# Masked attention: the query tiles in mixed order, the values' products in one stretch per two units

## The chip, the core and the metric

The kernel runs on one core of a Trainium2 chip. Its time is the device time of one execution in microseconds (us). Three runs took 3441.07, 3441.09 and 3444.06 us, median 3441.09.

Engines in this text: PE is the matrix engine, DVE the vector engine, ACT the engine for activations, POOL the general one, SP the one that issues DMAs. Each works through its own list of instructions in program order, and waits at semaphores that the others raise.

## The reference

The program is two layers over 1250 rows (nodes, later tokens) of 512 numbers: a graph sum, attention with a mixture of experts, a second graph sum, and a block with a temporal attention, a spatial attention, a cross attention and an MLP. Four attentions in all; the temporal one alone is masked:

```python
def _temporal_experts(xt, idx, qw, qb, kw, kb, vw, vb, pw, pb):
    B, T, _ = xt.shape                      # 1, 1250; H = 8 heads of HD = 64
    q = (jnp.einsum('btd,bod->bto', xt, qw[idx]) + qb[idx][:, None, :]).reshape(B, T, H, HD)
    ...
    logits = jnp.einsum('bthd,bshd->bhts', q, k) * HD ** (-0.5)
    causal = jnp.tril(jnp.ones((T, T), dtype=bool))
    logits = jnp.where(causal, logits, -jnp.inf)
    att = jax.nn.softmax(logits, axis=-1)
    o = jnp.einsum('bhts,bshd->bthd', att, v).reshape(B, T, D)
    o = jnp.einsum('btd,bod->bto', o, pw[idx]) + pb[idx][:, None, :]
    return xt + o
```

## The kernel before

`attention` is called four times, once with `causal=True`. After the projections it works through 80 units. A unit is one head and one tile of 125 queries; the heads go in 4 pairs, and a pair has 20 units. The order is in `units` (L593): for each pair, tiles two by two (0 and 1, then 2 and 3, ...), and for each two tiles both heads. So four units in a row see the same number of keys. Under the mask that number, `keys` (L594), is 2, 4, 6, 8 or 10 tiles of 125 keys, growing through the pair. Without the mask it is always 10.

Steps of a unit, and who takes them:
- PE multiplies queries and keys (`score_part`, L771 and L773, two products per piece). A unit has up to three pieces, in the order of `pieces` (L590). The scores of an even and of an odd unit lie in five banks, and share the middle one: an odd unit's last piece, and the last of an even unit with 10 tiles, wait for the exponential of the unit before (L770, `exp_done`).
- DVE adds the mask to the last one or two tiles (L960; 250 wide for an even unit, 125 for an odd one) and takes the maximum of the row (L962). Both are in `whole_max`. The stages without mask take most of the maximum ahead of time (`wide_max`, L968) and the last 226 columns later (`tail_max`, L975).
- ACT exponentiates with that maximum and sums up (L904).
- PE turns the result tile by tile (`turn_part`, L790), at most four tiles to a bank, which gives one, two or three turns per unit. ACT (L890) or DVE (L986) copies each turn to `p_t`; `by_act` says who.
- Two units next to each other (same head, two tiles) share one sum with the values: `duo_sum` (L807), for which one product of 250 columns per key tile is issued (the trace has two records for each). Even and odd key tiles go to the two halves of a bank. ACT copies the lower half (L914), DVE adds it to the upper and writes the output (L1008).

All engines step together through s = 0, 1, 2, ...: in step s PE makes the scores of unit s and turns units s-2 (or s-1), DVE takes the maximum of s-1 and its copies of s-2, ACT exponentiates s-1. When masked, each step holds two quarters of a sum between score pieces, and the half copy and the add come in odd steps (`sum_at`, L600). When not masked, PE works in two kinds of steps: an even one with turns and scores, and an odd one with scores, turns and then one whole sum ahead of the last score piece.

After a few units the sums of the exponentials are inverted (`norms`, L610: three times per pair), sent through DRAM to be spread over partitions (SP, L676 and L682), and POOL multiplies the output with them (`scale`, L712), the last time DVE.

Of the kernel before, what the change touches and what calls it, by code (L numbers as in the profile page):

```python
# [27 lines left out]
D = 512  # L28
TN = 125
NT = N // TN  # L30
DC = D // 128
# [11 lines left out]
HEADS = 8  # L43
# [458 lines left out]
def attention(nc, c, q_src, kv_src, out_t, wq_d, wk_d, wv_d, bq_d, bk_d, scratch, causal=False, pick=None, send=None,  # L502
# [10 lines left out]
    with ExitStack() as ctx:  # L513
# [76 lines left out]
        pieces = [[(0, 512), (512, 1024), (1024, N)], [(TAIL, TAIL + 512), (TAIL + 512, N), (0, TAIL)]]  # L590

        w_out = k_hi_both[:, :, :].rearrange("p h n -> p (h n)")[:, 0:DC * D].rearrange("p (k d) -> p k d", k=DC)
        units = [(j, h, i) for j in range(PAIRS_) for m in range(0, NT, 2) for h in range(2) for i in (m, m + 1)]  # L593
        keys = [(i // 2 * 2 + 2 if causal else NT) for _, _, i in units]  # L594
        turns = [-(-n // 4) for n in keys]
        upto = lambda u: sum(turns[:u])

        taken = [(u, n) for u in range(NU) for n in range(turns[u])]
        by_act = lambda u, n: (n == 0 or (n == 2 and u % 2 == 0)) if causal else (n == 2) == (u % 2 == 0)
        sum_at = lambda s: (s - 5) // 2 if causal and s % 2 == 1 else (s - 6) // 2 if not causal and s % 2 == 0 else -1  # L600
        act_by = lambda g: sum(1 for u, n in taken[:g] if by_act(u, n))
        dve_by = lambda g: g - act_by(g)

# [3 lines left out]
            if dve_by(g):  # L607
                eng.wait_ge(dve_took, dve_by(g))

        norms = [(j, k) for j in range(PAIRS_) for k in range(3)]  # L610
        n_units = lambda j, k: (UNITS * j + 8 * k, UNITS * j + min(8 * k + 8, UNITS))
        with stage(nc, "bias_in", "bias_set", "s_high", "s_low", "w_in0", "w_in1", "w_high", "w_low", "summed", "high",
                   "low", "saved", "first_in", "kq_in0", "kq_in1", "scored", "wide_scored", "wide_ready", "masked", "max_ready", "exp_done",
                   "turned", "act_took", "dve_took", "pv_done", "half_out", "added", "inv_made", "inv_out", "inv_in",
# [73 lines left out]
            @block.gpsimd  # L688
            def _(pool):
                if send is not None:  # L690
                    table_d, rows, slots = send

                def send_rows(a, b):
                    for t in range(a, b):
                        pool.indirect_dma_start(table_d, bass.IndirectOffsetOnAxis(ap=slots[:, t:t + 1], axis=0),  # L695
                                                rows[:, t, :], None).then_inc(sent, 16)

                first = 20 if send is not None else 0
                for n, (kind, last) in enumerate((("k", begin[1]), ("q", begin[5]))):
                    send_rows(first * n, first * (n + 1))  # L700
                    for r in range(RINGS):
                        pool.wait_ge(stored[r], stores_by(last, r))
                    load_pair(pool, 0, kind, first_in)

                def scale(x):
                    j, k = norms[x]
                    lo, hi = CHUNKS[k]
                    pool.wait_ge(inv_in, 32 * (x + 1))
                    pool.wait_ge(added, NT * j + min(4 * k + 4, NT))
                    dst = out_t[:, j, lo:hi].rearrange("q (i p) -> q i p", p=TN)  # L710
                    by = inverse_all[:, 0:hi - lo].rearrange("q (p i) -> q i p", p=TN)
                    pool.tensor_tensor(dst, dst, by, ALU.mult).then_inc(scaled, 1)  # L712

                early_norms = len(norms) - 3
                for x in range(len(norms) - 1):
                    if send is not None:
                        end = lambda n: 2 * first + (EC - 2 * first) * min(n, early_norms) // early_norms
                        send_rows(end(x), end(x + 1))
                    scale(x)
                pool.wait_ge(scaled, len(norms) - 1)  # L720
                if send is not None:
                    pool.wait_ge(sent, 16 * EC)

            @block.tensor
            def _(pe):
# [88 lines left out]
                for s in range(NU + 4):  # L814
                    if s == 2:

                        pe.wait_ge(low, len(items))
                    if causal:
                        quarter = 2 * (s % 2)
                        turn_part(s - 2, 0)  # L820
                        score_part(s, 0)
                        turn_part(s - 2, 1)
                        duo_sum((s - 4) // 2, quarter, quarter + 1)
                        score_part(s, 1)
                        turn_part(s - 2, 2)
                        duo_sum((s - 4) // 2, quarter + 1, quarter + 2)
                        score_part(s, 2)
                    elif s % 2 == 0:
                        turn_part(s - 2, 0)
                        turn_part(s - 2, 1)  # L830
                        score_part(s, 0)
                        score_part(s, 1)
                        turn_part(s - 2, 2)
                        turn_part(s - 1, 0)
                        score_part(s, 2)
                    else:
                        score_part(s, 0)
                        score_part(s, 1)
                        turn_part(s - 2, 1)
                        turn_part(s - 2, 2)  # L840
                        duo_sum((s - 5) // 2, 0, 4)
                        score_part(s, 2)

            @block.scalar
            def _(act):
# [46 lines left out]
                                   ACT.Copy).then_inc(act_took, 1)  # L892

                act.wait_ge(w_low, len(parts))
                for s in range(NU + 4 if causal else NU + 5):
                    take_part(s - 2, 0)
                    if 1 <= s <= NU:
                        t = s - 1
                        act.wait_ge(max_ready, t + 1)
                        if t >= 2:  # L900

                            act.wait_ge(turned, upto(t - 1))
                        w = TN * keys[t]
                        act.activation(p[:, t % 2, 0:w], score[t % 2][0:TN, 0:w], ACT.Exp,  # L904
                                       bias=neg_max[:, t:t + 1], accum_out=total[:, t:t + 1]).then_inc(exp_done, 1)
                    take_part(s - 2, 1)
                    take_part(s - 2, 2)
                    if sum_at(s) >= 0:
                        q = sum_at(s)
                        act.wait_ge(pv_done, q + 1)  # L910
                        if q >= 2:

                            act.wait_ge(added, q - 1)
                        act.activation(lower[:, q % 2, :], pout[64:128, 0:2 * TN], ACT.Copy).then_inc(half_out, 1)  # L914

            @block.vector
            def _(dve):
# [68 lines left out]
                    dve.tensor_copy(p_t[:, u // 2 % 2, 4 * n:4 * n + m, TN * (u % 2):TN * (u % 2) + TN],  # L986
                                    pturn[0:TN, g % 2, 0:TN * m].rearrange("p (a b) -> p a b", b=TN)).then_inc(dve_took, 1)

                for s in range(NU + 4 if causal else NU + 5):
                    if 1 <= s <= NU:  # L990
                        (whole_max if causal else tail_max)(s - 1)
                    u = s - 2
# [16 lines left out]
                                          lower[:, q % 2, :], ALU.add).then_inc(added, 1)  # L1009
                dve.wait_ge(added, NU // 2)  # L1010
                j, k = norms[-1]
                lo, hi = CHUNKS[k]
                dve.wait_ge(inv_in, 32 * len(norms))
                dst = out_t[:, j, lo:hi].rearrange("q (i p) -> q i p", p=TN)
                by = inverse_all[:, 0:hi - lo].rearrange("q (p i) -> q i p", p=TN)
# [1312 lines left out]
def program(nc, a, out):  # L2328
# [5 lines left out]
    with ExitStack() as ctx:  # L2334
# [26 lines left out]
        support, x1, z2 = (rows(n) for n in ("support", "x1", "z2"))  # L2361
        y_moe = dram("y_moe", [EXPERTS, CAP, D])
        scratch = (dram("q_parts", [2, HEADS // 2, 128, N]), dram("k_parts", [2, HEADS // 2, 128, N]),
                   dram("inverse", [3 * HEADS // 2, 2, 4 * TN]), dram("w_out", [128, DC, D]))
        hold = lambda: nc.sbuf_tensor(f"x_sb_{nc.next_id()}", [TN, NT, D], F32, side="right")
        with ExitStack() as layer0:
            s0 = lambda name, shape, dt=F32: layer0.enter_context(nc.sbuf_tensor(name, shape, dt))
# [132 lines left out]
```

## Time and profile before

| | |
|---|---|
| median of three runs | 3441.09 us |
| profiled execution, its span | 3439.76 us, 3437.5 us |
| busy share of the span: PE, DVE, ACT, POOL | 83%, 56%, 42%, 32% |
| mean granted PE clock | 0.928 of 2.4 GHz |
| HBM | 119 GB/s |
| exponentials, all attentions (L904) | 320, busy 383.8 us |
| turns by PE (L790), records | 2880, busy 433.6 us |
| products with the values (L807), records | 2880, busy 355.3 us |
| maxima of the masked stage (L962) | 80, 417 to 1460 ns |

The busy time of PE is modelled at its end, so that a PE that is marked busy need not be at its peak. A window's clock column is the mean of what was granted. In the timeline a row may stand for several instructions of one kind (x8); the number after the start is then the time from the first's start to the last's end.

### The profile page before, as it was taken

Reading aid. Unit: us, or ns where it says so; the run is one execution under the profiler, and the core shown is the slowest. Engines: PE = TensorE matmul, PEld = TensorE weight load, DVE = VectorE, ACT = ScalarE, POOL = GpSimd, SP = SyncE. Lnnn points to the kernel's source line nnn. Section 1 sums busy time; section 2 is a strip of 40 time slices with the busy share of each in tenths; the row PEclk is TensorE's granted clock in tenths of the full one; section 3 lists DMA queues with packets and bytes.
Section 4 is the critical chain, followed back from the end, with each engine's and each line's share of the span. In section 5 each row is a group of like instructions: output and inputs, shape, how many; then the busy total and the mean of one; then the engine's idle time right before and its main releaser. Section 6 shows DMA issues by size and latency. Waiting matters only on the chain. (4 is left out here: it accounts for less than half of the span.)

```text
span 3437.5 us, 46642 instructions
## 1 busy us (share of the span) xinstructions
PE 2854.2 (83%) x15398; PEld 1999.1 (58%) x15398; DVE 1925.7 (56%) x3890; ACT 1457.2 (42%) x3150; POOL 1115.2 (32%) x1138
## 2 busy tenths in 40 slices
PE   0403887999958995779999798989999999998899
PEld 0201227777756763434444585558777687776687
DVE  7203774577642114579999526653677636776544
ACT  0100003466604542556666435542566435665322
POOL 4777775467113433076665000000000000001220
PEclk9856998999968997989999899999999999999999
DMA  4104775533156994454443264214423044321322
GB/s 109 36 6 114 210 202 160 138 61 72 40 161 212 339 341 125 162 172 150 138 136 92 79 191 107 56 58 129 129 54 67 15 146 113 73 48 41 98 75 87
DMA packets 228769, 407.93 MB, mean 119 GB/s; under 512 B 48706, under 2 KB 146288, under 8 KB 224438
## 3 DMA queue, kind: packets, MB, share of 16 engines
q1 hardware_dynamic: 173222, 268.49, 27.3%
q0 software_dynamic: 54864, 136.39, 14.8%
q8 instruction: 127, 2.08, 0.3%
q14 instruction: 108, 0.88, 0.1%
q10 hardware_dynamic: 448, 0.08, 0.0%
HBM read 318.32 MB, written 90.35 MB: 119 GB/s over the span
## 5 line engine op out<-in xcount | busy, mean ns | idle before, releaser
L904 ACT ACTIVATE at_p<-at_pb,at_max 125x1250 f32<-125x1250 f32 (+4 forms) x320 | 383.8, 1199 | 302.0 <-DVE at_unused L975 273.3
L790 PE MATMUL at_pb<-ident,at_p 125*125 125x125 f32 x2880 | 433.6, 281 | 20.8 <-ACT at_p L904 17.6
L790 PEld LDWEIGHTS at_pb<-ident,at_p 125*125 125x125 f32 x2880 | 391.2, 191 | 83.7 <-ACT at_p L904 22.0
L807 PE MATMUL at_pb<-at_pt,at_v 125*64 125x250 f32 x2880 | 355.3, 383 | 5.2 <-DVE s_t L1008 3.0
L1457 PE MATMUL so_ps<-g_got,g_hot 128*125 128x512 f32 x332 | 177.5, 630 | 204.8 <-DMA g_got<-support,g_edges 172.0
L968 DVE TENSOR_REDUCE at_wide<-at_pb 125x1 f32<-125x1024 f32 x240 | 293.6, 1223 | 22.1 <-PE at_pb L773 3.8
L890 ACT ACTIVATE at_pt<-at_pb 125x500 f32<-125x500 f32 (+1 forms) x448 | 232.8, 520 | 97.4 <-PE at_pb L790 93.5
L712 POOL TENSOR_TENSOR s_t<-s_t,at_all 128x500 f32<-128x500 f32 (+1 forms) x33 | 42.7, 1293 | 656.2 <-DVE s_t L1008 656.0
L807 PEld LDWEIGHTS at_pb<-at_pt,at_v 125*64 125x64 f32 x2880 | 188.2, 137 | 104.1 <-issue 14.4
L750 PE MATMUL at_pb<-at_s,at_shared 128*128 128x500 f32 (+1 forms) x1152 | 229.2, 361 | 23.2 <-ACT at_shared L852 23.2
L986 DVE COPY at_pt<-at_pb 125x500 f32<-125x500 f32 (+1 forms) x416 | 232.4, 582 | 22.6 <-PE at_pb L790 22.6
L1457 PEld LDWEIGHTS so_ps<-g_got,g_hot 128*125 128x125 f32 x332 | 50.6, 187 | 331.7 <-issue 197.9
L695 POOL DMA_INDIRECT table<-rows,slots x160 | 197.9, 1237 | 95.7 <-issue 57.5
L750 PEld LDWEIGHTS at_pb<-at_s,at_shared 128*128 128x128 f32 x1152 | 196.0, 194 | 55.9 <-ACT at_shared L852 23.9
L1414 POOL DMA_INDIRECT table<-rows,slots x160 | 195.4, 1221 | 99.1 <-issue 99.1
L975 DVE TENSOR_SCALAR_CACHE_REDUCE at_unused<-at_pb,at_wide 125x226 bf16<-125x226 f32 x240 | 107.7, 449 | 205.3 <-PE at_pb L773 202.5
L2147 POOL DMA_INDIRECT g_got<-nodes,g_edges x176 | 176.9, 1005 | 133.7 <-DMA g_edges<-table 103.5
L2173 PE MATMUL g_pw<-g_w4two,g_h 128*128 128x512 f32 x352 | 181.4, 599 | 22.1 <-DMA g_h<-h_edges 17.7
L2184 PE MATMUL g_pm<-g_msg,g_hot 128*125 128x512 f32 x352 | 187.8, 615 | 14.3 <-DVE g_acc L2269 7.1
L771 PE MATMUL at_pb<-at_kh,at_q 128*125 128x512 f32 (+5 forms) x448 | 179.3, 407 | 20.0 <-ACT at_p L904 18.4
L2187 PE MATMUL g_pm<-g_msg,g_plain 128*125 128x512 f32 x352 | 181.4, 597 | 0.0
L771 PE MATMUL at_pb<-at_shared 128*125 128x512 f32 (+5 forms) x448 | 177.0, 402 | 3.9 <-ACT at_p L904 3.2
(320 smaller groups left out, 5505.7 us busy)
## 6 DMA issues: line engine op xcount, KB each, us to landing
w_ring<-in_L_ffn_w SPq DMA_DIRECT2D x128, 512.0 KB, 11.7
at_shared<-k_parts SPq DMA_DIRECT2D x64, 312.5 KB
ml_w<-in_mlp_w SPq DMA_DIRECT2D x64, 256.0 KB
k_parts<-at_shared SPq DMA_DIRECT2D x64, 250.0 KB, 2.9
q_parts<-at_shared SPq DMA_DIRECT2D x64, 250.0 KB, 3.4
h_edges<-em_both SPq DMA_DIRECT2D x11, 1024.0 KB, 3.9
g_h<-h_edges SPq DMA_DIRECT2D x11, 1024.0 KB, 5.6
at_shared<-q_parts SPq DMA_DIRECT2D x32, 312.5 KB
```

Source lines behind the costliest of these rows:

```text
L695: pool.indirect_dma_start(table_d, bass.IndirectOffsetOnAxis(ap=slots[:, t:t + 1], axis=0), rows[:, t, :], None).then_inc(sent, 16)
L750: ins = pe.matmul(bank[:, (x + 6) % 8, 0:s.stop - s.start], a[:, ci % 2, k, 128 * (j % 2):128 * (j % 2) + 128], b[:, k, s], start=(t == 0) ...
L771: pe.matmul(score[u % 2][0:TN, a:b], q_two[j % 2][h][:, TN * i:TN * i + TN], k_hi[j % 2][h][:, a:b], start=True, stop=False)
L790: ins = pe.transpose(pturn[0:TN, g % 2, TN * (t % 4):TN * (t % 4) + TN], p[:, u % 2, TN * t:TN * t + TN], c.ident[0:TN, 0:TN])
L807: ins = pe.matmul(pout[side:side + 64, 0:2 * TN], v[:, t, 2 * j + h, :], p_t[:, q % 2, t, :], start=(t < 2), stop=(t >= keys[u] - 2))
L890: act.activation(p_t[:, u // 2 % 2, 4 * n:4 * n + m, TN * (u % 2):TN * (u % 2) + TN], pturn[0:TN, g % 2, 0:TN * m].rearrange("p (a b) -> p ...
L904: act.activation(p[:, t % 2, 0:w], score[t % 2][0:TN, 0:w], ACT.Exp, bias=neg_max[:, t:t + 1], accum_out=total[:, t:t + 1]).then_inc(exp_d ...
L968: dve.tensor_reduce(neg_wide[:, u:u + 1], score[u % 2][0:TN, a:a + 1024], AX, ALU.max, negate=True)\
L986: dve.tensor_copy(p_t[:, u // 2 % 2, 4 * n:4 * n + m, TN * (u % 2):TN * (u % 2) + TN], pturn[0:TN, g % 2, 0:TN * m].rearrange("p (a b) -> ...
L1414: pool.indirect_dma_start(self.table_d, bass.IndirectOffsetOnAxis(ap=self.slots[:, t:t + 1], axis=0), self.rows[:, t, :], None).then_inc(s ...
L1457: pe.matmul(ps[0:TN, 4 + i % 4, :], self.hot[:, i % HOT, :], self.got[:, i % RING, :], start=True, stop=True)\
L2184: pe.matmul(pm[0:TN, 2 * (q % 2), :], hot[:, t % MR, :], msg[:, t % MR, 0:4, :].rearrange("p a b -> p (a b)"), start=not second, stop=bool ...
```

## The change

Only for the masked attention the order of the query tiles becomes 8, 0, 6, 2, 4, so that the key tiles per unit go 10, 2, 8, 4, 6 in groups of four units. The masked stage drops its own order of steps and takes that of the others: whole sums in odd steps, the half copy and the add in even steps, and copies dealt by `(n == 2) == (u % 2 == 0)`: of an even unit DVE copies the turns 0 and 1 and ACT turn 2, of an odd unit the reverse. Each group has an inversion of its own, five per pair, and the number of steps is one more on ACT and DVE. For the other three attentions the lists come out as they were.

```diff
-        units = [(j, h, i) for j in range(PAIRS_) for m in range(0, NT, 2) for h in range(2) for i in (m, m + 1)]
+        groups = [(8,), (0,), (6,), (2,), (4,)] if causal else [(0, 2), (4, 6), (8,)]
+        order = [m for g in groups for m in g]
+        units = [(j, h, i) for j in range(PAIRS_) for m in order for h in range(2) for i in (m, m + 1)]
...
-        by_act = lambda u, n: (n == 0 or (n == 2 and u % 2 == 0)) if causal else (n == 2) == (u % 2 == 0)
-        sum_at = lambda s: (s - 5) // 2 if causal and s % 2 == 1 else (s - 6) // 2 if not causal and s % 2 == 0 else -1
+        by_act = lambda u, n: (n == 2) == (u % 2 == 0)
+        sum_at = lambda s: (s - 6) // 2 if s % 2 == 0 else -1
...
-        norms = [(j, k) for j in range(PAIRS_) for k in range(3)]
-        n_units = lambda j, k: (UNITS * j + 8 * k, UNITS * j + min(8 * k + 8, UNITS))
+        norms = [(j, k) for j in range(PAIRS_) for k in range(len(groups))]
+        until = lambda k: sum(len(g) for g in groups[:k])
+        n_units = lambda j, k: (UNITS * j + 4 * until(k), UNITS * j + 4 * until(k + 1))
+        n_columns = lambda k: (TN * groups[k][0], TN * (groups[k][-1] + 2))
...
-                    lo, hi = CHUNKS[k]
+                    lo, hi = n_columns(k)
...
-                    pool.wait_ge(added, NT * j + min(4 * k + 4, NT))
+                    pool.wait_ge(added, NT * j + 2 * until(k + 1))
...
-                    if causal:
-                        quarter = 2 * (s % 2)
-                        turn_part(s - 2, 0)
-                        score_part(s, 0)
-                        turn_part(s - 2, 1)
-                        duo_sum((s - 4) // 2, quarter, quarter + 1)
-                        score_part(s, 1)
-                        turn_part(s - 2, 2)
-                        duo_sum((s - 4) // 2, quarter + 1, quarter + 2)
-                        score_part(s, 2)
-                    elif s % 2 == 0:
+                    if s % 2 == 0:
...
-                for s in range(NU + 4 if causal else NU + 5):
+                for s in range(NU + 5):
```

The same names as above stand in the instruction lists; the lines of the changed kernel are 6 lower on DVE and 4 higher on PE. DVE before, in the 8-tile units: mask (250 wide is an even unit's), maximum, copy of a turn, add.

```order
L960 TENSOR_TENSOR at_pb<-at_pb,causal 125x125
L962 TENSOR_REDUCE at_max<-at_pb 125x1
L986 COPY at_pt<-at_pb 125x4x125
L960 TENSOR_TENSOR at_pb<-at_pb,causal 125x250
L962 TENSOR_REDUCE at_max<-at_pb 125x1
L986 COPY at_pt<-at_pb 125x4x125
L1008 TENSOR_TENSOR t_t<-at_pb,at_lower 64x250
L960 TENSOR_TENSOR at_pb<-at_pb,causal 125x125
L962 TENSOR_REDUCE at_max<-at_pb 125x1
```

DVE in the changed kernel, in the 8-tile units:

```order
L954 TENSOR_TENSOR at_pb<-at_pb,causal 125x250
L956 TENSOR_REDUCE at_max<-at_pb 125x1
L954 TENSOR_TENSOR at_pb<-at_pb,causal 125x125
L956 TENSOR_REDUCE at_max<-at_pb 125x1
L980 COPY at_pt<-at_pb 125x4x125 x2
L1002 TENSOR_TENSOR t_t<-at_pb,at_lower 64x250
L954 TENSOR_TENSOR at_pb<-at_pb,causal 125x250
L956 TENSOR_REDUCE at_max<-at_pb 125x1
```

The add (`t_t<-at_pb,at_lower`) stood ahead of the mask of an odd unit (125 wide) and stands ahead of that of an even one (250 wide), behind the even unit's two copies.

PE before, in the first 2-tile units of a pair, behind the 10-tile ones (`ident` rows are turns, `at_pt,at_v` products with the values, 24 and 226 wide rows the scores of an odd 2-tile unit):

```order
L790 MATMUL at_pb<-ident,at_p 125x125 x4
L771 MATMUL at_pb<-at_shared 125x24
L773 MATMUL at_pb<-at_shared 125x24
L790 MATMUL at_pb<-ident,at_p 125x125 x4
L807 MATMUL at_pb<-at_pt,at_v 64x250 x4
L771 MATMUL at_pb<-at_shared 125x226
L773 MATMUL at_pb<-at_shared 125x226
L790 MATMUL at_pb<-ident,at_p 125x125 x2
L807 MATMUL at_pb<-at_pt,at_v 64x250 x2
```

PE in the changed kernel at the same place:

```order
L775 MATMUL at_pb<-at_kh,at_q_24098 125x24
L777 MATMUL at_pb<-at_kl,at_q_24098 125x24
L775 MATMUL at_pb<-at_kh,at_q_24098 125x226
L777 MATMUL at_pb<-at_kl,at_q_24098 125x226
L794 MATMUL at_pb<-ident,at_p 125x125 x6
L811 MATMUL at_pb<-at_pt,at_v 64x250 x10
L794 MATMUL at_pb<-ident,at_p 125x125 x2
L775 MATMUL at_pb<-at_kh,at_q_24099 125x250
L777 MATMUL at_pb<-at_kl,at_q_24099 125x250
L794 MATMUL at_pb<-ident,at_p 125x125 x2
```

The ten products of a 10-tile sum stood in pieces of two and four between the scores; now they stand in one row, and the scores of the next unit behind them.

## Rows read from the trace of the kernel before

**Rows 1.** Timeline of ACT: exponentials; start us, us, line, operation, [idle before <-releaser]
```profile
2056.23 0.47 ACT L904 ACTIVATE at_p<-at_pb,at_max 125x250 f32<-125x250 f32 x1 [1.39 <-DVE at_max L962]
...
2112.25 0.47 ACT L904 ACTIVATE at_p<-at_pb,at_max 125x250 f32<-125x250 f32 x1
...
2122.57 0.67 ACT L904 ACTIVATE at_p<-at_pb,at_max 125x500 f32<-125x500 f32 x1
...
2133.74 0.88 ACT L904 ACTIVATE at_p<-at_pb,at_max 125x750 f32<-125x750 f32 x1
...
2144.68 1.09 ACT L904 ACTIVATE at_p<-at_pb,at_max 125x1000 f32<-125x1000 f32 x1
...
2150.72 1.09 ACT L904 ACTIVATE at_p<-at_pb,at_max 125x1000 f32<-125x1000 f32 x1
...
2157.99 1.30 ACT L904 ACTIVATE at_p<-at_pb,at_max 125x1250 f32<-125x1250 f32 x1 [0.87 <-DVE at_max L962]
...
2172.57 0.46 ACT L904 ACTIVATE at_p<-at_pb,at_max 125x250 f32<-125x250 f32 x1
...
2289.61 1.30 ACT L904 ACTIVATE at_p<-at_pb,at_max 125x1250 f32<-125x1250 f32 x1 [0.92 <-DVE at_max L962]
```

**Rows 2.** Windows: length, busy us of PE PEld DVE ACT POOL, PEclk, DMA, GB/s
```profile
2113.00:2173.00 60.00, 53.83 (x328) 35.08 (x326) 35.97 (x68) 33.58 (x72) 3.72 (x3) 0.94 0.37 76
2123.20:2133.20 10.00, 8.54 (x39) 5.91 (x38) 5.17 (x11) 4.62 (x13) 0.00 (x0) 0.70 1.03 219
2450.00:2700.00 250.00, 250.00 (x1820) 195.83 (x1819) 182.91 (x360) 161.26 (x280) 12.70 (x10) 1.00 0.22 48
```

**Rows 3.** Timeline between two exponentials, 8-tile unit, then a 10-tile one
```profile
2091.61 0.38 ACT L914 ACTIVATE at_lower<-at_pb 64x250 f32<-64x250 f32 x1
...
2092.02 0.41 DVE L1008 TENSOR_TENSOR t_t<-at_pb,at_lower 64x250 f32<-64x250 f32 x1 [0.57 <-ACT at_lower L914]
...
2092.36 0.28 DVE L960 TENSOR_TENSOR at_pb<-at_pb,causal 125x125 f32<-125x125 f32 x1
...
2092.67 1.20 DVE L962 TENSOR_REDUCE at_max<-at_pb 125x1 f32<-125x1000 f32 x1
...
2093.90 1.10 ACT L904 ACTIVATE at_p<-at_pb,at_max 125x1000 f32<-125x1000 f32 x1 [0.66 <-DVE at_max L962]
...
2095.20 0.37 PE L771 MATMUL at_pb<-at_kh,at_q 128*125 128x226 f32 x1
...
2095.71 0.43 DVE L960 TENSOR_TENSOR at_pb<-at_pb,causal 125x250 f32<-125x250 f32 x1 [1.26 <-PE at_pb L773]
...
2096.17 1.46 DVE L962 TENSOR_REDUCE at_max<-at_pb 125x1 f32<-125x1250 f32 x1
```

**Rows 4.** Groups by form, 2053 to 2302 us: busy, mean ns, idle before
```profile
L890 ACT ACTIVATE at_pt<-at_pb 125x500 f32<-125x500 f32 x64 | 37.8, 590 | 55.4 <-PE at_pb L790 55.4
...
L986 DVE COPY at_pt<-at_pb 125x500 f32<-125x500 f32 x32 | 21.5, 671 | 8.4 <-PE at_pb L790 8.4
```

**Rows 5.** Timeline of PE in the next, unmasked attention stage
```profile
2472.31 2.33 PE L807 MATMUL at_pb<-at_pt,at_v 125*64 125x250 f32 x20
...
2474.57 0.37 PE L771 MATMUL at_pb<-at_kh,at_q 128*125 128x226 f32 x1
...
2474.89 1.04 PE L790 MATMUL at_pb<-ident,at_p 125*125 125x125 f32 x8
...
2475.68 0.48 PE L771 MATMUL at_pb<-at_kh,at_q 128*125 128x512 f32 x1
...
2476.71 1.01 PE L790 MATMUL at_pb<-ident,at_p 125*125 125x125 f32 x6
```

**Rows 6.** Timeline of SP at the causal stage's end
```profile
2294.17 0.26 SPq L676 DMA_DIRECT2D inverse<-at_inv  x1
```

**Rows 7.** Timeline of ACT and DVE in the unmasked stage
```profile
2477.59 0.38 ACT L914 ACTIVATE at_lower<-at_pb 64x250 f32<-64x250 f32 x1
...
2478.05 0.40 DVE L1008 TENSOR_TENSOR s_t<-at_pb,at_lower 64x250 f32<-64x250 f32 x1
```

More of the change, by code:

```diff
@@ L987, in take_part @@
                                     pturn[0:TN, g % 2, 0:TN * m].rearrange("p (a b) -> p a b", b=TN)).then_inc(dve_took, 1)
-                for s in range(NU + 4 if causal else NU + 5):
+                for s in range(NU + 5):
                     if 1 <= s <= NU:
@@ L1011, in _ @@
                 j, k = norms[-1]
-                lo, hi = CHUNKS[k]
+                lo, hi = n_columns(k)
                 dve.wait_ge(inv_in, 32 * len(norms))
@@ L2363, in program @@
         scratch = (dram("q_parts", [2, HEADS // 2, 128, N]), dram("k_parts", [2, HEADS // 2, 128, N]),
-                   dram("inverse", [3 * HEADS // 2, 2, 4 * TN]), dram("w_out", [128, DC, D]))
+                   dram("inverse", [NT // 2 * HEADS // 2, 2, 4 * TN]), dram("w_out", [128, DC, D]))
         hold = lambda: nc.sbuf_tensor(f"x_sb_{nc.next_id()}", [TN, NT, D], F32, side="right")
```

## The prediction

> **What bounds the kernel now.** The order of reading was: the page's slices, to see that no engine is full over the whole span; then one stretch of the causal attention by windows; then its exponentials in the timeline; then the rows between two exponentials. The page's chain of waits ends in the MLP and says nothing here.
>
> Only one of the four attention stages changes: the causal one. For the others the new lists give the same order (0, 2, 4, 6, 8) in the same three groups. So the question is how long 80 units take. The first exponential starts at 2056.23 and the last at 2289.61: 233.38 us [rows 1]. A middle pair takes 60.32 us, from 2112.25 to 2172.57, split by the starts of its groups: the four 2-tile units 10.32 us, 4-tile 11.17, 6-tile 10.94, 8-tile 13.31, 10-tile 14.58. "n-tile" means n key tiles.
>
> In such a pair PE is marked busy for 53.8 of 60 us, DVE 36.0, ACT 33.6 [rows 2]. None is full: a serial loop sets the pace. [Rows 3] shows it for 8-tile units. ACT copies the lower half of a finished sum (2091.61), DVE adds it (2092.02), masks the next scores (2092.36), takes the maximum (2092.67, 1.20 us), ACT exponentiates (2093.90, 1.10 us). Then PE writes the last piece of the next unit's scores (2095.20), since that piece shares a bank with the unit just exponentiated; mask follows 0.51 us later. DVE and ACT work in program order, so whatever stands between two maxima on DVE is in the loop, if it is late.
>
> **Sizes used.** Exponential E = 0.47, 0.67, 0.88, 1.10, 1.30 us for 2, 4, 6, 8, 10 tiles [rows 1, 3]. Maximum M = 1.20 for 8, 1.46 for 10 tiles [rows 3], so 0.26 per two tiles: 0.94, 0.68, 0.42 for the smaller.
>
> **Part 1: copies by even and odd units, the add in even steps.** On each engine the new stream of steps is the one that the other three stages already have; they differ in the maximum. Before, the half copy and the add stand ahead of an odd unit's maximum, where DVE would wait for the last piece of scores anyway. Now they stand ahead of an even unit's maximum, behind the exponential of the odd unit (first order excerpt).
> - Odd unit now: exponential, 0.15 until the last piece (0.20 in [rows 3], where PE had other work until then), 0.51 to the mask, 0.31 to the maximum, M, 0.03. That is E + M + 1.00: 3.30 us for 8 tiles. Before it was 1.10, some 0.10 for reading out the sum, and 2.29 from the half copy to the next exponential: 3.49.
> - Even unit now: E + 0.10, half copy and add 0.75, mask 0.46 (0.15 more than the short one), M, 0.03, that is E + M + 1.34: 3.64 us for 8 tiles. Before, from start to start, 6.04 us per two (2144.68 to 2150.72), so 2.55 for it. Two units: 6.94 against 6.04.
> - For 10 tiles ACT also copies the even unit's third turn ahead of the half copy, 0.40: 1.30 + 1.46 + 1.34 + 0.40 = 4.50; odd 3.76. Without the add it would still be 4.40: the last piece now stands behind four transposes (0.49).
>
> DVE takes on 16 four-tile copies at 0.671 us (10.7 us) that cost ACT 0.590 (9.4) [rows 4]. For even 6- and 8-tile units both copies (0.67 + 0.41, or 1.34) lie beside the odd exponential and half copy (0.98 + 0.4, or 1.20 + 0.4), so I cost them at nothing there. In the 2- and 4-tile groups they are not covered; they are in part 2. Two more reciprocals a pair (0.17 us each) stand after an odd step's copies; hidden except once per pair. SP gets 8 more rounds of three inverse DMAs and POOL 20 products for 12: SP's wait for each round is shorter than the 12 us between two, the loads of a pair's keys and queries stand ahead of a pair's first round as before, and POOL is busy 3.7 of 60 us [rows 2]. Nothing.
>
> **Part 2: the values' products in one stretch, in mixed order.** A 10-tile sum in one stretch takes 2.26 us on PE (2472.31 to 2474.57, in a stage that has this order already) [rows 5]; scaled by the number of products, 8 tiles take 1.87 with a start of 0.1. Transposes: 0.125 each at 8 per 1.04; two 512-wide score pieces about 1.0 (2475.68 to 2476.71). In the new order the sums of the 10-tile units stand in the 2-tile group (second order excerpt), those of the 8-tile ones in the 4-tile group. Small units wait for them. From the start C of the first 2-tile exponential:
> - its end 0.62; last piece 0.55; six transposes 0.85; products 2.33: C + 4.35. Meanwhile the second unit, behind DVE's copy of the last turn (0.42), reciprocal, mask and maximum, starts at C + 3.4.
> - third unit: transposes and copy 0.72, add 0.38, mask 0.44, maximum and gap 0.45: C + 6.34. Its end and the last piece of the fourth begin at C + 6.96; products until C + 9.84.
> - first 8-tile unit: transposes 0.25, its scores 1.0, mask, maximum 1.20: C + 12.8.
>
> So this group takes 12.8 us against 10.32. The 4-tile group, by the same steps from K: last piece K + 0.82, 0.55, transposes 0.50, products until 3.74; transposes 0.5, copy 0.67, add 0.38, mask 0.44, maximum 0.68: third unit K + 6.5; fourth's last piece 7.3, products until 9.75, then 0.55 + 0.67 + 0.38 + 0.44 + 0.97: K + 12.75, against 11.17.
>
> The other groups, up to the first unit of the next: 10-tile 3.76 + 4.50 + 3.76 + 3.46 = 15.48 (14.58 before); 8-tile 3.30 + 3.64 + 3.30 + 3.12 = 13.36 (13.31); 6-tile 2.82 + 3.16 + 2.82 + 3.98 = 12.78 (10.94), the last being the step into a 10-tile unit behind four transposes.
>
> **The sum.** A pair: 12.8 + 13.36 + 12.75 + 12.78 + 15.48 = 67.2 us. First to last exponential: 4 x 67.17, less the 3.98 into the first unit and 0.1 for the third unit, which has no add before it: 264.6 us, 31.2 more. Start: the first maximum is over 10 tiles, 1.46 for 0.42: +1.0. End: before, the last inverse leaves at 2294.17, 4.56 us after the last exponential began, behind a 10-tile remainder; now 0.98 + 0.40 + 0.41 + 0.2 = 2.0, and the DMAs and the last product follow as before [rows 6]: -2.5. Together +29.7.
>
> **The clock.** I used full-clock durations. Before, a middle pair has a mean granted clock of 0.94, and the 4-tile group 0.70 [rows 2]: about 2 x 0.06 x 60 = 7.2 us at 1.2 GHz, in which PE does 3.6 us of work too slowly. If it falls as much now and all of it were in the loop, 4 x 3.6 = 14 us come on top; if none, 0. Before, it is in a group of small units that it fell; now the two small groups hold 8.4 us of dense products, so I take 3. The Trainium skill, "TensorE: Matmul & The Clock Gate", section "Loop structure matters more than you think", says that back-to-back matmuls keep the clock up, and it counts for this change: by it the 3 fall away and the kernel ends at 3471 us. The stage without gaps on PE, 250 of 250 us busy at 1.00 [rows 2], agrees; none of its rows shows what PE's gaps of some 2 us beside the small units will do.
>
> Profiled: 3439.76 + 32.7 = 3472.5. The median of the runs is 1.33 us above the profiled one: **3474 us**.
>
> **Rivals.**
> - *The mixing hides what it should.* Small units run in the shadow of the large ones' products, so that only the loops E + M + 1.00 and E + M + 1.34 are left: 10-tile 16.5, 8-tile 13.9, 6-tile 12.0, 4-tile 10.1, 2-tile 8.2, 60.7 a pair: 4 x 60.7 - 4.1 = 238.7, +5.3, with the ends +3.8, 3445. For it: PE's 53.8 busy us hold waits. Against: the products are ahead of the next unit's scores in PE's order, and 2.33 us is more than a small unit's whole loop.
> - *Faster, by the clock.* The same, and the clock stays at 1.00: 4 x 3.6 = 14 us back, 3431. It decides where PE is in the loop at low clock, which the 4-tile group's 11.17 us for 10.1 makes possible. Against: the even unit's add is late by the order alone.
> - *Slower still, by the clock.* PE idles some 2 us before each small unit's last piece. If the clock falls there, the products that follow double: 2 x 2.33 + 2 x 1.87 = 8.4 us a pair, +34, 3508.
> - *No change* could come if the add were not in the loop and the boundary waits were those of now; the stage with this order shows the add at 2478.05 after the half copy at 2477.59 [rows 7], late behind the odd exponential. I count it with the first rival.
>
> **How the numbers follow.** Forecast 0.82 (own range 3458 to 3490: 2 us a pair either way for the waits I could not see, and the clock's 0 to 14), first rival 0.05, faster rival 0.04, slower rival 0.09. Range 3452 to 3496: it leaves out most of the slower rival, the two rivals below, and the forecast's own tails, together about 0.2. What this measurement can tell from no change is about 0.2%, 7 us. Slower 0.91, same 0.05, faster 0.04.
>
> **What would show it.** In the changed profile: a middle pair of 67 us from exponential to exponential; 8-tile units alternating 3.3 and 3.6 us instead of 3.5 and 2.5; ahead of an even unit's mask DVE's add, and its idle time put down to the half copy of ACT; runs of 20 product records beside 2-tile units, with the next scores behind them; the first 8-tile exponential some 4.5 us after the last 2-tile one. It would be wrong if even units keep 2.5 us, if the 2-tile group takes 10 us or less, or if the clock column of the small groups leaves the range 0.7 to 1.0.

## The result, and the profile after

The changed kernel takes 3495.59 us (median of 4 runs, 3494.01 to 3499.01), the kernel before 3441.08 in the same comparison (3431.85 to 3444.06). By these medians it is slower by 54.5 us, a ratio of 1.0158; over the single runs of both the ratio is 1.0165, 95% interval 1.0153 to 1.0177. The profiled execution took 3496.39 us, 56.6 more than before. The forecast was 3474, the range ended at 3496. The direction was right, but the forecast had only 33 of the 55 us.

Profile after, timeline of ACT: the first and the last exponential of the masked stage, and the first of each group of four in the second pair. These answer to [rows 1].

```profile
2056.37 1.30 ACT L898 ACTIVATE at_p<-at_pb,at_max 125x1250 f32<-125x1250 f32 x1 [2.43 <-DVE at_max L956]
...
2126.51 1.30 ACT L898 ACTIVATE at_p<-at_pb,at_max 125x1250 f32<-125x1250 f32 x1 [1.52 <-DVE at_max L956]
...
2141.77 0.47 ACT L898 ACTIVATE at_p<-at_pb,at_max 125x250 f32<-125x250 f32 x1 [0.49 <-DVE at_max L956]
...
2158.80 1.09 ACT L898 ACTIVATE at_p<-at_pb,at_max 125x1000 f32<-125x1000 f32 x1 [1.04 <-DVE at_max L956]
...
2172.18 0.68 ACT L898 ACTIVATE at_p<-at_pb,at_max 125x500 f32<-125x500 f32 x1 [0.49 <-DVE at_max L956]
...
2189.33 0.89 ACT L898 ACTIVATE at_p<-at_pb,at_max 125x750 f32<-125x750 f32 x1 [0.68 <-DVE at_max L956]
...
2202.13 1.30 ACT L898 ACTIVATE at_p<-at_pb,at_max 125x1250 f32<-125x1250 f32 x1 [1.52 <-DVE at_max L956]
...
2348.51 0.89 ACT L898 ACTIVATE at_p<-at_pb,at_max 125x750 f32<-125x750 f32 x1 [1.60 <-DVE at_max L956]
```

From first to last it is 292.14 us, for 233.38 before; the sum had 264.6. A middle pair takes 75.62 us (2126.51 to 2202.13), where the prediction named 67 as a sign. The groups of the second pair take 15.26 (10-tile), 17.03 (2-tile), 13.38 (8-tile), 17.15 (4-tile) and 12.80 (6-tile). The forecast said 15.48, 12.8, 13.36, 12.75 and 12.78. Three of five are right within 0.25 us; both groups of small units are over 4 us too short in it.

Windows by those groups (length, busy us of PE, PEld, DVE, ACT, POOL, then the granted clock, DMA, GB/s), answering to [rows 2]:

```profile
2126.51:2141.77 15.26, 10.33 (x70) 7.55 (x66) 9.59 (x16) 8.80 (x16) 0.67 (x1) 1.00 0.71 145
2141.77:2158.80 17.03, 14.56 (x74) 9.41 (x74) 5.80 (x15) 4.35 (x13) 0.79 (x2) 0.70 0.58 112
2158.80:2172.18 13.38, 7.44 (x48) 5.64 (x48) 8.78 (x16) 7.16 (x14) 0.73 (x1) 1.00 0.11 10
2172.18:2189.33 17.15, 14.57 (x76) 9.76 (x76) 6.40 (x14) 5.49 (x14) 0.73 (x1) 0.70 0.09 9
2189.33:2202.13 12.80, 9.59 (x66) 7.21 (x66) 8.35 (x16) 6.11 (x13) 0.74 (x1) 1.00 0.08 11
```

The clock column tells the two kinds apart: 1.00 in the three groups that came out as worked out, 0.70 in the other two. The DMA column doesn't: the two slow groups have 0.58 and 0.09 in it. Nor does PE's share of busy time: the 8-tile group has 7.44 of 13.38 us at 1.00.

The steady loop, timeline of ACT and DVE for two 8-tile units, the odd one first; [rows 3] is the same place before:

```profile
2162.12 1.10 ACT L898 ACTIVATE at_p<-at_pb,at_max 125x1000 f32<-125x1000 f32 x1 [2.13 <-DVE at_max L956]
...
2163.33 0.38 ACT L908 ACTIVATE at_lower<-at_pb 64x250 f32<-64x250 f32 x1
...
2163.74 0.41 DVE L1002 TENSOR_TENSOR t_t<-at_pb,at_lower 64x250 f32<-64x250 f32 x1 [0.48 <-ACT at_lower L908]
...
2164.07 0.41 DVE L954 TENSOR_TENSOR at_pb<-at_pb,causal 125x250 f32<-125x250 f32 x1
...
2164.52 1.20 DVE L956 TENSOR_REDUCE at_max<-at_pb 125x1 f32<-125x1000 f32 x1
...
2165.75 1.09 ACT L898 ACTIVATE at_p<-at_pb,at_max 125x1000 f32<-125x1000 f32 x1 [1.00 <-DVE at_max L956]
```

Here the mechanism stands as forecast. The even unit's exponential begins 3.63 us after the odd one's (3.64 in the sum), and between them lie the half copy, the add, the mask and the maximum, one behind the other.

Timeline of PE at the second 2-tile unit, where the sum of 10-tile units stands; [rows 5] is such a sum at full clock:

```profile
2140.46 0.26 PE L777 MATMUL at_pb<-at_shared 128*125 128x24 f32 x1
...
2142.39 0.55 PE L775 MATMUL at_pb<-at_shared 128*125 128x226 f32 x1 [1.67 <-ACT at_p L898]
...
2142.94 1.49 PE L794 MATMUL at_pb<-ident,at_p 125*125 125x125 f32 x6
...
2144.36 4.35 PE L811 MATMUL at_pb<-at_pt,at_v 125*64 125x250 f32 x20
...
2148.64 0.48 PE L794 MATMUL at_pb<-ident,at_p 125*125 125x125 f32 x2
```

PE waits 1.67 us for the exponential, writes the last piece, makes six turns in 1.4 us, and then the 20 records of the sum take 4.35 us. At full clock they took 2.33. Windows of 2 us over the same place, with the columns of before:

```profile
2139.00:2141.00 2.00, 1.28 (x8) 1.02 (x8) 1.04 (x3) 1.80 (x5) 0.00 (x0) 1.00 1.02 210
2141.00:2143.00 2.00, 0.61 (x3) 0.62 (x4) 0.70 (x2) 0.84 (x3) 0.72 (x1) 0.67 1.05 225
2143.00:2145.00 2.00, 2.00 (x11) 1.61 (x12) 0.54 (x3) 0.59 (x1) 0.00 (x0) 0.50 0.98 210
2145.00:2147.00 2.00, 2.00 (x14) 1.10 (x12) 0.57 (x2) 0.56 (x2) 0.00 (x0) 0.50 1.09 238
2147.00:2149.00 2.00, 2.00 (x13) 0.99 (x10) 0.00 (x0) 0.24 (x1) 0.00 (x0) 0.63 1.00 206
```

The clock falls to 1.2 GHz (0.50) while PE waits and does not come back until the sum is nearly over. The next sum, at the fourth 2-tile unit, has a gap of 1.62 us ahead of it, takes 4.02 us and again runs mostly at 0.50. But not every such gap is followed by the low clock. At the same place of the first pair the gap is 1.63 us and the sum takes 2.33 us; the window 2078.71 to 2086.12 is at 1.00:

```profile
2080.34 0.37 PE L775 MATMUL at_pb<-at_kh,at_q 128*125 128x226 f32 x1 [1.63 <-ACT at_p L898]
...
2080.74 2.33 PE L811 MATMUL at_pb<-at_pt,at_v 125*64 125x250 f32 x20
```

So in this kernel too the same sum at the same place is fast when the clock is up.

The last inverse, timeline of SP, answering to [rows 6]:

```profile
2350.56 0.26 SPq L680 DMA_DIRECT2D inverse<-at_inv  x1
```

It leaves 2.05 us after the last exponential began, for 4.56 before; the sum had 2.0.

### The profile page after: what moved, and what is told of

It reads as the page before. It is cut to its first block and busy times, and to the rows that moved or that the text cites. A ratio compares the mean times of both kernels' runs of the same rounds, so it can differ in the third digit from the quotient of the medians.

```text
span 3494.3 us, 46685 instructions
## 1 busy us (share of the span) xinstructions
PE 2863.9 (82%) x15398; PEld 2017.0 (58%) x15398; DVE 1938.8 (55%) x3914; ACT 1449.6 (41%) x3134; POOL 1115.4 (32%) x1146
## 5 line engine op out<-in xcount | busy, mean ns | idle before, releaser
L811 PE MATMUL at_pb<-at_pt,at_v 125*64 125x250 f32 x2880 | 362.9, 400 | 4.1 <-DVE s_t L1002 3.0
L980 DVE COPY at_pt<-at_pb 125x500 f32<-125x500 f32 (+1 forms) x432 | 240.9, 585 | 70.2 <-PE at_pb L794 70.2
L811 PEld LDWEIGHTS at_pb<-at_pt,at_v 125*64 125x64 f32 x2880 | 203.7, 144 | 111.0 <-issue 25.9
L884 ACT ACTIVATE at_pt<-at_pb 125x500 f32<-125x500 f32 (+1 forms) x432 | 223.1, 517 | 74.7 <-PE at_pb L794 71.1
L775 PE MATMUL at_pb<-at_kh,at_q 128*125 128x512 f32 (+7 forms) x448 | 175.3, 399 | 40.5 <-ACT at_p L898 40.2
L775 PE MATMUL at_pb<-at_shared 128*125 128x512 f32 (+7 forms) x448 | 173.7, 395 | 24.5 <-ACT at_p L898 24.5
```

The source lines that it names most:

```text
L775: pe.matmul(score[u % 2][0:TN, a:b], q_two[j % 2][h][:, TN * i:TN * i + TN], k_hi[j % 2][h][:, a:b], start=True, stop=False)
L811: ins = pe.matmul(pout[side:side + 64, 0:2 * TN], v[:, t, 2 * j + h, :], p_t[:, q % 2, t, :], start=(t < 2), stop=(t >= keys[u] - 2))
L884: act.activation(p_t[:, u // 2 % 2, 4 * n:4 * n + m, TN * (u % 2):TN * (u % 2) + TN], pturn[0:TN, g % 2, 0:TN * m].rearrange("p (a b) -> p ...
```

## The experiments

All times but two, which are marked as one run, are medians beside the kernel before, which took 3439.5 to 3440.3 us in these comparisons. "A 2-tile group" is the time from the first exponential of four 2-tile units to the first of the next group.

**The mixed order alone.** The old steps of the masked stage are put back, the order stays:

```diff
-                    if s % 2 == 0:
+                    if causal:
+                        quarter = 2 * (s % 2)
...
+                        duo_sum((s - 4) // 2, quarter, quarter + 1)
...
+                    elif s % 2 == 0:
```

> The mixed order of query tiles alone: the masked stage keeps its old steps (quarters of a sum between score pieces, half copy and add in odd steps, old dealing of copies). Theory (the loss is the even units' late add, and the whole sums that run at half clock behind PE's gaps): neither is here, so most of the 56 us are not there: 3445 to 3455 us, a pair 60 to 62 us from exponential to exponential. Rival (the mixed order itself costs it, since small units stand behind large ones): 3475 us or more.

Measured: 3446.79 us, ratio 1.0024 (1.0014 to 1.0033). First to last exponential 238.9 us, a middle pair 60.8. The window of a 2-tile group (columns as above):

```profile
2127.49:2137.93 10.44, 9.36 (x61) 5.28 (x60) 5.65 (x14) 4.41 (x16) 0.00 (x0) 1.00 0.92 195
```

The order costs 7 us and no more. Of the 5.5 us from first to last exponential 4.4 are in the first pair (60.4 us for 56.0), where the old order began with 2-tile units that had no sum of larger units beside them (7.53 us for the group, 10.32 later); a middle pair takes 60.8 for 60.3. The clock is at 1.00 in every group: with quarters of a sum between score pieces and turns, PE's gaps in a middle pair are at most 1.27 us.

**The new steps alone.** Query tiles in the old order:

```diff
-        groups = [(8,), (0,), (6,), (2,), (4,)] if causal else [(0, 2), (4, 6), (8,)]
+        groups = [(0,), (2,), (4,), (6,), (8,)] if causal else [(0, 2), (4, 6), (8,)]
```

> The new steps alone: query tiles in the old order 0, 2, 4, 6, 8, five groups per pair. Theory: even units' loop E + M + 1.34 in all groups, and one slow group per pair (2-tile, with the sums of the 10-tile units at half clock, some 16.5 us where 12.3 were at full clock). First to last exponential 251 us at full clock, 264 with the half clock, for 233 before: 3470 us, 3457 if the clock stays. Rival (it is the mixed order): 3441 to 3448 us.

Measured: 3469.65 us, ratio 1.0089 (1.0073 to 1.0106). First to last exponential 262.3 us. The 2-tile group behind the 10-tile one:

```profile
2122.51:2138.32 15.81, 12.52 (x66) 8.33 (x66) 5.18 (x15) 4.35 (x13) 0.77 (x2) 0.71 0.49 99
```

Both parts of the loss are there with the steps alone: even units of 3.16 (6 tiles), 3.63 (8) and 4.37 us (10), and one slow group in each of the pairs 2 to 4 (15.1 to 15.9 us, 0.71 to 0.77). The 4-tile group has 0.84 there and takes 10.4 to 10.7 us. The two single effects, 30 and 7 us, do not make up the 55: together order and steps give a second slow group per pair, the 4-tile one with the 8-tile sums.

**The gap filled with products.** Ahead of the first score piece of an odd 2- or 4-tile unit, six products of 512 columns go into banks of the same unit:

```diff
+                    if causal and n == 0 and u % 2 and keys[u] <= 4:
+                        for _ in range(6):
+                            pe.matmul(score[1][0:TN, TAIL:TAIL + 512], q_two[j % 2][h][:, TN * i:TN * i + TN],
+                                      k_hi[j % 2][h][:, TAIL:TAIL + 512], start=True, stop=True)
```

> The changed kernel with PE's gap filled: ahead of the first score piece of each odd 2- and 4-tile unit six products of 512 columns are added, into a part of the same unit's score banks that is written again or not read. They need about 1.3 us at full clock, in a gap of 1.7 us. Clock theory: the granted clock of the small groups goes from 0.70 towards 1.0, a 20-record sum from 4.3 us to 2.3, the 2-tile group from 17.0 to 12.8 to 14 us and the 4-tile one from 17.1 to 12.8 to 14: 3467 to 3475 us. Rival (the stretch of products is slow for a reason of its own, such as its place or its reads): sums stay at 4.3 us, time 3495 us or some us more.

Measured: 3470.36 us, ratio 1.0095 (1.0078 to 1.0111), 25 us below the changed kernel with more work on PE. Timeline of PE at the same place (the added products, the last piece, the sum), then the window of the group:

```profile
2139.31 1.64 PE L777 MATMUL at_pb<-at_shared 128*125 128x512 f32 x6
...
2141.34 0.37 PE L779 MATMUL at_pb<-at_shared 128*125 128x226 f32 x1 [0.27 <-ACT at_p L902]
...
2142.41 2.33 PE L815 MATMUL at_pb<-at_pt,at_v 125*64 125x250 f32 x20
```

```profile
2140.73:2153.14 12.41, 11.68 (x83) 8.26 (x82) 5.80 (x15) 4.33 (x13) 0.07 (x1) 1.00 0.71 151
```

The 20 records take 2.33 us for 4.35, the 2-tile group 12.41 (the sum of the prediction had 12.8), the 4-tile group 12.58 (12.75), the latter in all four pairs. The 2-tile groups of pairs 1 and 3 took 13.91 and 13.14, at 0.92 and 0.97: there the clock had fallen in the 10-tile group ahead. First to last exponential: 263.98, where the prediction had 264.6.

**The same gap, filled with narrow products.** 24 columns in place of 512:

> As the run with the filled gap, but the six added products have 24 columns instead of 512, so that PE gets the same number of instructions and about a twentieth of the columns. Clock theory: the small groups stay near 0.70 and 16.5 to 17 us each. Rival (any instruction in the gap helps, or it was the wait's place and not the work): as with 512 columns, 12.4 to 12.6 us each.

Measured, in one run: 3489.35 us. Timeline of PE and window of the group as above:

```profile
2138.03 0.80 PE L777 MATMUL at_pb<-at_shared 128*125 128x24 f32 x6
...
2140.06 0.55 PE L779 MATMUL at_pb<-at_shared 128*125 128x226 f32 x1 [1.01 <-ACT at_p L902]
...
2142.03 4.32 PE L815 MATMUL at_pb<-at_pt,at_v 125*64 125x250 f32 x20
```

```profile
2139.45:2156.44 16.99, 15.18 (x80) 10.03 (x80) 5.79 (x15) 4.33 (x13) 0.78 (x2) 0.70 0.57 116
```

The same number of instructions, but 1.0 us of gap is left and the clock falls as without them: 4.32 us for the sum. Not every group was as slow as expected: one 2-tile group took 14.03 at 0.88, and 4-tile groups took 14.2 to 15.5. So six instructions in the gap are not enough; they have to fill it. This run doesn't tell whether it is the columns or the length of the gap left (1.0 us against 0.27) that counts, nor how much is needed.

**The last piece set free.** A smaller even unit does not use the shared bank, and the wait is left out there:

```diff
-                    if u >= 1 and a == (0 if u % 2 else 1024):
+                    if u >= 1 and a == (0 if u % 2 else 1024) and TN * keys[u - u % 2] > 1024:
```

> The changed kernel, but the last score piece of an odd unit waits for the exponential of the unit before only where that one has 10 key tiles (a smaller even unit does not use the shared bank). PE's gap before the small units' last piece goes, and the odd exponential no longer stands behind the even one. Theory: two 8-tile units go from 6.94 to 5.2 us, two 6-tile ones from 6.0 to 4.5; the small groups fall to about 10.5 us each if the clock comes back, else 14 to 15; all in all 3423 us (3410 to 3435), or 3455 at half clock in the small groups. Rival (the last piece is not in the loop, the add alone is): within 5 us of 3495.

Measured: 3422.74 us, ratio 0.9952 (0.9935 to 0.9968). ACT's exponentials of 8-tile units (odd one second), then the window of a 2-tile group:

```profile
2136.78 1.09 ACT L898 ACTIVATE at_p<-at_pb,at_max 125x1000 f32<-125x1000 f32 x1 [1.03 <-DVE at_max L956]
...
2138.56 1.10 ACT L898 ACTIVATE at_p<-at_pb,at_max 125x1000 f32<-125x1000 f32 x1 [0.59 <-DVE at_max L956]
...
2142.19 1.09 ACT L898 ACTIVATE at_p<-at_pb,at_max 125x1000 f32<-125x1000 f32 x1 [1.00 <-DVE at_max L956]
```

```profile
2127.78:2136.78 9.00, 8.96 (x69) 6.44 (x68) 5.70 (x15) 4.23 (x13) 0.04 (x1) 1.00 0.94 204
```

The odd 8-tile unit follows the even one by 1.78 us (2.03 in the group's second two) for 3.32, the even one still takes 3.63, its add being where it was. The gaps ahead of the sums are gone and the clock is back at 1.00 in the small groups: 9.00 us for 17.03. The two edits that take PE's gap away in opposite ways, by filling it and by removing its wait, both bring the clock back.

**The half copy ahead of the exponential.** On ACT, in even steps:

```diff
                     take_part(s - 2, 0)
+                    if causal:
+                        half(s)
                     if 1 <= s <= NU:
```

> The changed kernel with one instruction moved on ACT in the masked stage: the half copy of an even step stands ahead of the odd unit's exponential instead of behind it. Theory (the add is in the loop of even units because the half copy waits for that exponential): the even 8-tile unit goes from 3.63 to 3.3 us, the 6-tile one from 3.16 to 2.9 (DVE's two copies, add, mask and maximum are next), the 10-tile one stays at 4.37 (there it is the last piece behind four turns). Some 5 us less, 3490. Rival (the add was never late; PE or the copies set the even unit): all three stay.

Measured, in one run: 3472.18 us. Exponentials of 8-tile units:

```profile
2154.04 1.09 ACT L909 ACTIVATE at_p<-at_pb,at_max 125x1000 f32<-125x1000 f32 x1 [1.03 <-DVE at_max L962]
...
2157.35 1.09 ACT L909 ACTIVATE at_p<-at_pb,at_max 125x1000 f32<-125x1000 f32 x1 [1.73 <-DVE at_max L962]
...
2160.41 1.09 ACT L909 ACTIVATE at_p<-at_pb,at_max 125x1000 f32<-125x1000 f32 x1 [0.43 <-DVE at_max L962]
```

The odd unit stays at 3.31, the even one falls from 3.63 to 3.06, the 6-tile one from 3.16 to 2.53, and the 10-tile one stays (4.35). That the half copy behind the exponential set the even unit is shown; its size was underestimated (3.3 and 2.9 expected), as DVE's two copies come in less time (1.25 us) than two times 0.67. Of the 21.7 us less than the changed kernel from first to last exponential, the 8- and 6-tile groups give 1.04 + 0.63 a pair, the 10-tile ones 0.7 in all four pairs together (0.61 in two of them, 0.6 longer in the first), some 7.4; the other 14.3 are in the small groups, which came at clocks of 0.70 to 1.00 here (12.6 to 17.1 us).

**Both together.**

> The changed kernel with the free last piece and the half copy ahead of the exponential. Theory: two 8-tile units 4.85 us instead of 5.67, two 6-tile ones 4.2 instead of 5.1, the 10-tile ones unchanged, small groups within 0.5 us: 3408 us (3402 to 3415), for 3423 with the free piece alone. Rival (half copies that wait for a late sum now hold the exponentials of the small groups up): small groups 1 us longer each, 3416 or more.

Measured: 3429.48 us, ratio 0.997 (0.996 to 0.9979): 7 us above the free piece alone. The rival was right. Two 8-tile units take 5.15, but an exponential of a small unit now stands behind a half copy that waits for a late sum. Timeline of ACT, the half copy and the exponential of a 2-tile unit whose maximum was ready 2.3 us before:

```profile
2133.75 0.38 ACT L895 ACTIVATE at_lower<-at_pb 64x250 f32<-64x250 f32 x1 [2.87 <-PE at_pb L811]
2134.15 0.47 ACT L909 ACTIVATE at_p<-at_pb,at_max 125x250 f32<-125x250 f32 x1
```

The 2-tile group takes 10.2 us at a clock of 1.00 and 11.3 to 11.8 in the three pairs in which the clock fell, for 9.0; the 4-tile group 9.42 for 8.5.

**The kernel before with the free last piece.**

> The kernel before, with the free last piece alone. Theory: there the odd unit's mask stands behind the half copy, which stands behind the even unit's exponential, so that the loop of 3.49 us stays for 8 and 6 tiles; only small groups gain: 3432 to 3441 us. Rival (the last piece's wait is the loop there too): as much as in the changed kernel, 1.7 us per two 8-tile units, 3400 to 3415.

Measured: 3435.16 us, ratio 0.9985 (0.9975 to 0.9995). 8-tile units stay at 3.49 and 2.52 us. In the old steps the odd unit's mask is held by the add as well, and taking one of two waits of nearly equal length away frees little.

**Free last piece, and in even steps the last piece ahead of the odd unit's turns.**

> The changed kernel with the free last piece and the last score piece ahead of the turns in even steps, the half copy as in the change. By the loops of the prediction a 10-tile even unit has 4.50 by the add and 4.40 by the piece behind the turns, so that taking the second away alone leaves it where the add puts it: 4.3 to 4.4 us as now; the step from 6 to 10 tiles goes from 3.94 to 3.5: 3420 us. Rival (the turns ahead of the piece were all of it): 3.95 us, 3416.

Measured: 3423.31 us, ratio 0.9949 (0.9933 to 0.9964). Exponentials of 10-tile units in the second pair; the third is an even one:

```profile
2113.10 1.30 ACT L902 ACTIVATE at_p<-at_pb,at_max 125x1250 f32<-125x1250 f32 x1 [1.05 <-DVE at_max L960]
...
2116.89 1.30 ACT L902 ACTIVATE at_p<-at_pb,at_max 125x1250 f32<-125x1250 f32 x1 [2.12 <-DVE at_max L960]
...
2121.26 1.30 ACT L902 ACTIVATE at_p<-at_pb,at_max 125x1250 f32<-125x1250 f32 x1 [1.32 <-DVE at_max L960]
```

The even unit stays at 4.37. In the first pair, where there is no add yet, it takes 3.91. So the add and the piece behind the turns were two waits of one length, as the prediction had them (4.50 and 4.40). The step from 6 to 10 tiles fell from 3.94 to 3.68 only, where 3.5 was expected, and two 2-tile groups took 11.2 and 10.5 us at 0.86 and 0.92, so that the time is that of the free piece alone.

**The three edits together**, the half copy early only ahead of 8- and 10-tile exponentials:

```diff
+                def early_half(s):
+                    return causal and 1 <= s <= NU and keys[s - 1] >= 8
...
-                        turn_part(s - 1, 0)
-                        score_part(s, 2)
+                        score_part(s, 2)
+                        turn_part(s - 1, 0)
```

(the second part for the masked stage only)

> The changed kernel with the free last piece, the half copy ahead of the exponential only where that is of an 8- or 10-tile unit, and in even steps the last score piece ahead of the four turns of the odd unit. From the periods measured: 10-tile group 13.8 us (4.37 to 3.95 twice), 2-tile 9.0, 8-tile 10.1, 4-tile 8.5, 6-tile 10.8 (the step into the 10-tile unit 3.45 for 3.94): 52.2 a pair, first to last exponential 205 us for 233 before, 3410 us (3405 to 3417). Rival (the score piece ahead only delays the turns, and DVE's copies then bind): 10-tile group as now, 3415 to 3420.

Measured: 3419.46 us, ratio 0.9944 (0.993 to 0.9957), the fastest measured here. The 10-tile units again:

```profile
2108.42 1.30 ACT L916 ACTIVATE at_p<-at_pb,at_max 125x1250 f32<-125x1250 f32 x1 [1.05 <-DVE at_max L969]
...
2112.20 1.30 ACT L916 ACTIVATE at_p<-at_pb,at_max 125x1250 f32<-125x1250 f32 x1 [1.72 <-DVE at_max L969]
...
2116.12 1.30 ACT L916 ACTIVATE at_p<-at_pb,at_max 125x1250 f32<-125x1250 f32 x1 [0.86 <-DVE at_max L969]
```

Now the even one takes 3.92. The time is 9 us above what was expected: 2-tile groups took 9.6 us, and 11.1 and 11.2 in two pairs at a clock of 0.85, where 9.0 were counted; the 4-tile group took 8.97 (8.5 counted) and the 10-tile one 14.2 (13.8). From the free piece alone (3422.7) it is 3 us away.

**The same with the old order of tiles.**

> The same three edits with the query tiles in the old order 0, 2, 4, 6, 8. Theory (the mixed order gives nothing of its own: it makes three crossings into smaller units per pair instead of one): about 51 us a pair, 3405 to 3412 us, no slower than with the mixed order. Rival (mixing hides PE's large sums beside small units once no unit waits for an exponential it does not need): 3418 us or more.

Measured: 3420.88 us, ratio 0.9948 (0.9935 to 0.9962), above the time expected and in the rival's range, but not to be told from the mixed order's 3419.46. So no gain of the mixed order shows once the waits are gone.

## Why the prediction was right or wrong

**Right: the loop.** "E + M + 1.34" and "E + M + 1.00" gave 3.64 and 3.30 us for 8 tiles; the trace has 3.63 and 3.32. For 6 tiles 3.16 and 2.82 against 3.16 and 2.85, for 10 tiles 4.50 and 3.76 against 4.37 and 3.79. That the even unit's half copy and add are in it is shown by the run that moves the half copy.

**Right: the waits of small units behind whole sums.** With the gap filled and the clock at 1.00, the two groups take 12.41 and 12.58 us where part 2 had 12.8 and 12.75.

**Right: the end** (2.05 us for 2.0). Whether the start's 1.0 was right can't be told: the first exponential begins at 2056.37, 0.14 later than before, but in the other runs it begins anywhere from 2052.5 to 2061.9.

**Wrong: the clock term.** The text took 3 us, between 0 and 14; the clock cost some 28. With the gap filled, the stage takes 263.98 us from first to last exponential, and 292.14 without the filling. It was mis-sized both in its value and in its upper end. In pairs 2 to 4 the small groups take 25.0 us more than worked out, in the first pair 3.3: 28.3 together, for the 27.5 us by which the stage is longer than the sum (the 10-tile groups give 0.2 a pair back). Two steps of the reasoning failed. The upper end, 4 x 3.6 us, was taken from how much PE lost to the clock before, but the change puts 8.4 us a pair of other work, all of it in the loop, where the clock falls; the end should have been the 34 us that the slower rival had, as what was lost before said nothing of them. And the choice of 3 rested on "the two small groups hold 8.4 us of dense products", which was an argument for a high clock in the wrong order of time: the gap of 1.7 us comes first, and the products behind it pay. The slower rival named exactly this, the gap and the doubled sums, and was given 0.09. It had 3508, 12 us too much: 5 of them in the first pair, whose sums ran partly at full clock, and 3 because it put its 34 us on top of the forecast's own 3.

The section of the Trainium skill that was weighed says that back-to-back matmuls keep the clock up ("TensorE: Matmul & The Clock Gate", "Loop structure matters more than you think"). The filled gap agrees with it: the same sums ran at 1.00 when products stood ahead of them. The 3471 us that the prediction drew from it did not come, as PE's work was not back to back: behind the gap the sum ran at 0.50 until it was nearly over.

**Not so: that mixing hides something.** The rival with 3445 us needed small units to run in the shadow of the sums. PE works in program order, and the scores of the next unit stand behind the sum.

**Open.** How much work in a gap holds the clock isn't settled, nor why one gap is followed by the low clock and another of the same length (1.63 us in the first pair, 1.47 and 1.50 in the 8-tile groups) is not: the same group of the same kernel took 14.2 or 17.1 us in different pairs, and with narrow products 14.0 to 17.0. Whether a shorter sum in two halves would do as well as the old quarters with the new dealing of copies wasn't tried.

## What to carry to other kernels

Dense work put behind a wait can cost what it takes at the low clock: where a sum moves into units shorter than itself, look at PE's gap ahead of it, and let the upper end of the range be all of what follows at half clock. In a loop over engines in program order, a small copy or add costs little or its full length, by whether it stands ahead of a wait that is there anyway. Twice here two waits of nearly equal length stood in one place (the odd unit before, the 10-tile even unit after), and removing one showed little or nothing. The gain was elsewhere: a wait for a bank that the unit before does not use held every odd unit of fewer than 10 tiles, and leaving it out of the changed kernel took it from 3495.6 to 3422.7 us, below the kernel before.

## What the runs showed of the hardware

In a gap of 1.67 us on PE, with PE marked busy 1.28 of the 2 us just before, the granted clock fell to 0.50, and 4.35 us of products without a pause then ran at it nearly to the end (0.50, 0.50, 0.63 in windows of 2 us). Two units later a gap of 1.62 us was followed by 4.02 us for the 20 records of a sum; at the same place of the first pair a gap of 1.63 us passed at 1.00, and such a sum took 2.33 us behind it. With six products of 512 columns ahead of the gap's piece the clock did not fall there (the group at 1.00, 12.41 us), with six of 24 columns it did (0.70, 16.99 us). Two copies of 125 x 500 one behind the other take 1.25 us on DVE for a single one's 0.67.
